# Routing in two phases: batches 0 to 3 inside attention's last groups, batches 4 to 7 behind it

## What is computed

```python
x = x + relu(xattn(layernorm(x), ctx, ctx) @ wo_w.T + wo_b)   # 16 heads of 16, 375 keys
xf = layernorm(x)                                             # 896 tokens x 256
scores = softmax(xf @ gw + gb)                                # 32 experts
group_scores = sum(top_k(scores.reshape(T, 8, 4), 2)[0])      # per group of 4 experts
keep = the 4 best groups
indices = top_k(where(keep, scores, -inf), 4)[1]              # 4 experts per token
weights = take_along_axis(scores, indices)
for e in range(32):
    h = silu(xf @ w1[e] + b1[e]) * (xf @ w3[e] + b3[e])
    y += cw[:, e] * (h @ w2[e] + b2[e])
z = silu(xf @ sw1 + sb1) * (xf @ sw3 + sb3) @ sw2 + sb2       # shared expert, 256 wide
return x + y + z
```

## Time and profile before

| | |
|---|---|
| time, median of 3 runs | 343.71 us (343.64 to 344.85) |
| the profiled execution: its run | 342.33 us |
| its span, first to last instruction | 340.6 us |
| PE busy | 300.8 us (88%) |
| DVE busy | 192.6 us (57%) |
| ACT busy | 158.0 us (46%) |
| POOL busy | 157.1 us (46%) |
| mean granted clock of PE | 0.94 |

### The profile page before, as it was taken

One profiled execution on the slowest core, in us unless ns is written; L12 is line 12 of the kernel. 1 busy time (PEld: TensorE's weight loads), 2 busy tenths in 40 slices (PEclk: granted clock), 3 DMA queues, 4 the chain that ended last, 5 costly groups with the idle time before them and its releaser, 6 DMA issues.

```text
span 340.6 us, 7222 instructions
## 1 busy us (share of the span) xinstructions
PE 300.8 (88%) x2311; PEld 209.3 (61%) x2311; DVE 192.6 (57%) x679; ACT 158.0 (46%) x426; POOL 157.1 (46%) x222
## 2 busy tenths in 40 slices
PE   7899999999999999899499646399999999999965
PEld 3566666666666677564445333267777777787543
DVE  2899766565656567178750301067876666666343
ACT  5566666666666656525011011045556665555101
POOL 7564444444444445001037777126555555555600
PEclk9999999999999999997679955599999999999999
DMA  7999596959786700008803333655544554553498
GB/s 193 214 155 307 164 315 191 297 146 318 228 250 195 244 2 2 0 2 243 253 28 100 110 113 111 107 110 181 156 149 150 162 157 154 162 158 107 129 295 210
DMA packets 56941, 55.92 MB, mean 164 GB/s; under 512 B 19165, under 2 KB 49386, under 8 KB 56394
## 3 DMA queue, kind: packets, MB, share of 16 engines
q1 hardware_dynamic: 52538, 43.94, 48.7%
q0 software_dynamic: 4368, 11.52, 10.3%
HBM read 35.03 MB, written 20.41 MB: 163 GB/s over the span
## 4 chain that ended last, share of the span: by engine, by line
PE 28%; POOL 9%; DVE 7%; DMA 5%; issue 4%; ACT 1%; DVEq 0%; SPq 0%; POOLq 0%
PE ps L961 13%; POOL expert_rows L879 9%; PE ps L976 6%; PE ps L953 3%; DMA b<-expert_out 2%; PE ps L970 2%; DMA expert_out<-hs,to 1%; PE ps L1016 1%; DMA expert_rows<-normed,slots 1%; DMA xg<-expert_rows 1%; POOL expert_out L884 1%; DVE hb L1234 1%; ACT sg L1050 1%; DVE hh L1240 1%; PE ps L924 1%
## 5 line engine op out<-in xcount | busy, mean ns | idle before, releaser
L607 DVE CUSTOM_DVE_ANT_0 z<-ps,mask_sb 112x375 f32<-112x375 f32 x128 | 62.5, 546 | 43.3 <-PE ps L390 43.2
L313 POOL TENSOR_SCALAR z<-z,zmax 112x375 f32<-112x375 f32 x96 | 55.7, 594 | 67.0 <-DVE zmax L607 67.0
L884 POOL DMA_INDIRECT expert_out<-hs,to x59 | 56.7, 961 | 51.2 <-DVE hs L1206 36.3
L513 ACT ACTIVATE pT<-ps 125x336 f32<-125x336 f32 x128 | 50.7, 448 | 38.5 <-PE ps L367 38.2
L961 PE MATMUL ps<-w,xgT 128*128 x236 | 65.6, 403 | 3.0 <-ACT xgT L1040 3.0
L367 PE MATMUL ps<-ident,z 112*125 112x112 f32 x384 | 56.6, 283 | 0.2 <-ACT pT L513 0.2
L367 PEld LDWEIGHTS ps<-ident,z 112*125 112x125 f32 x384 | 47.3, 188 | 14.9 <-ACT pT L513 7.3
L1234 DVE TENSOR_TENSOR hb<-ps,b 128x256 f32<-128x256 f32 x59 | 25.1, 425 | 52.0 <-PE ps L961 48.8
L961 PEld LDWEIGHTS ps<-w,xgT 128*128 128x128 f32 x236 | 43.9, 198 | 14.7 <-issue 6.7
L879 POOL DMA_INDIRECT expert_rows<-normed,slots x32 | 30.3, 947 | 29.4 <-DVE normed L1183 20.0
L1056 ACT COPY hs<-ps 128x128 f32<-128x128 f32 x59 | 15.6, 265 | 47.4 <-PE ps L970 47.4
(11 more groups left out here) (181 smaller groups left out, 346.0 us busy)
## 6 DMA issues: line engine op xcount, KB each, us to landing
xg<-expert_rows SPq DMA_DIRECT2D x59, 128.0 KB, 2.3
expert_rows<-zero SPq DMA_DIRECT2D x14, 512.0 KB, 10.1
w2s<-in_L_ffn_w SPq DMA_DIRECT2D x2, 2048.0 KB, 9.2
b<-in_L_ffn_b SPq DMA_DIRECT2D x2, 2048.0 KB, 13.2
ctx_sb<-in_ctx SPq DMA_DIRECT2D x8, 336.0 KB
b<-expert_out SPq DMA_DIRECT2D x6, 448.0 KB, 6.4
mask_sb<-in_mask_Bx1xSxS_ff SPq DMA_DIRECT2D x8, 164.1 KB, 2.3
expert_out<-hs,to POOLq DMA_INDIRECT x59, 2.8
```

The costliest lines, as they stand in the source:

```text
L313: pool.tensor_scalar(z[:, n % RING, :], z[:, n % RING, :], -1.0, zmax[:, n % RING:n % RING + 1], ALU.mult, ALU.add).then_inc(by_pool, 1)
L513: nc.scalar.activation(pT[:, n % RING, :], ps[0:KP, T_BANK + at % 2, 0:KT * S], ACT.Exp).then_inc(ring_read, 1)
L607: nc.vector.tensor_tensor_reduce(out=z[:, n % RING, :], in0=ps[0:S, S_BANK + j, 0:SK], in1=mask_sb[:, b % 2, :], scale=-1.0, scalar=BIG, o ...
L884: pool.indirect_dma_start(ys, bass.IndirectOffsetOnAxis(ap=to[:, j:j + 1], axis=0), y_sb[:, j % 4, :], None).then_inc(y_sent[j % 4], 16)
```

## The change

Routing is split into phase 0 (batches 0 to 3) and phase 1 (batches 4 to 7), with tiles of half the width.

- Phase 0 runs in attention. DVE takes mean and variance with the Newton steps in group 20 and normalises four batches in group 21; PE turns them as two ring units at the end of group 22 (`xT0`, `xT1`) and makes the logits as a third in 23; DVE's routing steps are dealt over groups 24 to 31, with ACT's exp in group 25; ranks and counts are a fourth unit at the end of group 31. Behind group 32's residual DVE makes blocks, keys and slots of phase 0.
- POOL issues 8 of the 16 scatters of phase 0 ahead of the barrier, 8 behind it. Its constants are made in group 5, DVE's tables in group 7.
- Phase 1 runs in `experts`. Its rows first fill what is free in an expert's last block of phase 0 (`room`) and then go to further blocks (`more_blocks`, `more_keys`). The number of blocks in the loop, 59, stays. A block's owner is the sum of two parts, one for each phase.
- `x_sb` is now the same tile as `x2`, and `wo_raw`, `b1r`, `b3r` lie in `xf`.

```diff
+    PHASES = ((0, B // 2), (B // 2, B))
+    PB = B // 2
+    ROUTED_AT = (("xT0", 22), ("xT1", 22), ("logit", 23), ("rank", 31))
+    EXP_AT = 25
+    FIRST_ROWS = 8
...
     def closing(p):
         b, r = p // QPB, p % QPB
+        units = []
         if p < NQ and r < 3 and b + 1 < B:
-            return [(("k0", "k1", "q")[r], b + 1)]
+            units.append((("k0", "k1", "q")[r], b + 1))
         if p < NQ and r == 3 and b:
-            return [("ctxT", b - 1)]
-        return []
+            units.append(("ctxT", b - 1))
+        return units + [(kind, 0) for kind, at in ROUTED_AT if at == p]
...
+        def more_blocks(chained, counts):
+
+            chained(nc.vector.scalar_tensor_tensor(base1[:], held[:], -1.0, counts, ALU.add, ALU.add))
+            chained(TT(over[:], base1[:].unsqueeze(2).to_broadcast([P, E, LIM]),
+                       full[:].unsqueeze(1).to_broadcast([P, E, LIM]), ALU.is_gt))
+            chained(nc.vector.tensor_reduce(blocks[:], over[:], AX.X, ALU.add))
+            chained(TT(shift[:], blocks[:], had[:], ALU.subtract))
+            chained(nc.vector.tensor_tensor_scan(ends[:], ones_e[:], shift[:], 0.0, ALU.mult, ALU.add))
+            chained(nc.vector.tensor_scalar(free[:, 1:2], ends[:, E - 1:E], -1.0, free[:, 0:1], ALU.mult, ALU.add))
+            chained(nc.vector.tensor_scalar(ends[:], ends[:], free[:, 1:2], None, ALU.add))
+            chained(TT(shift[:], ends[:], blocks[:], ALU.subtract))
+            nc.vector.scalar_tensor_tensor(base1[:], shift[:], float(PART), held[:], ALU.mult, ALU.add)
+            chained(nc.vector.scalar_tensor_tensor(tail1[:], shift[:], -float(PART), tail1[:], ALU.mult, ALU.add))
+
+        def more_keys(chained, ranks):
+            lo, hi = PHASES[1]
+            chained(TT(msc[:], ranks, every(room[:]), ALU.is_lt))
+            TT(msc[:], msc[:], every(tail1[:]), ALU.mult)
+            chained(TT(key[:, lo:hi, :], ranks, every(base1[:]), ALU.add))
+            chained(TT(key[:, lo:hi, :], key[:, lo:hi, :], msc[:], ALU.add))
+            chained(TT(key[:, lo:hi, :], key[:, lo:hi, :], sel[:, lo:hi, :].bitcast(F32), ALU.mult))
...
+        def place(chained, f):
+            lo, hi = PHASES[f]
+            sort_best(chained, f, key[:, lo:hi, :])
+            nc.vector.tensor_scalar(slots[:, lo:hi, :], best[:, lo:hi, 0:TOPK], -1.0, None, ALU.add).then_inc(slots_ok, 1)
+            nc.vector.tensor_scalar(normed[:, lo:hi, D:D + TOPK], best[:, lo:hi, 0:TOPK], -1.0, None, ALU.add).then_inc(slots_ok, 1)
...
+        def rank_and_count(f, ranks, counts):
+
+            lo, hi = PHASES[f]
+            nc.tensor.matmul(ranks, earlier[:, 0:ranks.shape[0]], sel[:, lo:hi, :].rearrange("s b e -> s (b e)"), start=True, stop=True)
+            for b in range(PB - 1):
+                ins = nc.tensor.matmul(ranks[:, (b + 1) * E:PB * E].rearrange("s (b e) -> s b e", e=E), ones[:, 0:ranks.shape[0]],
+                                       sel[:, lo + b:lo + b + 1, :].to_broadcast([S, PB - 1 - b, E]), start=False,
+                                       stop=True, skip_group_check=True)
+            ins.then_inc(ranked, 1)
+            for b in range(lo, hi):
+                ins = nc.tensor.matmul(counts, ones[:], sel[:, b, :], start=(b == lo), stop=(b == hi - 1))
+            return ins
...
+        EARLY_ROWS = [(r, b) for r in reversed(range(TOPK)) for b in range(*PHASES[0])]
...
+                    elif p == QPB + 1:
+                        routing_constants()
+                pool.wait_ge(slots_ok, 2)
+                pool.wait_ge(xs_zero, 16 * (N_ZERO + 1))
+                for r, b in EARLY_ROWS[:FIRST_ROWS]:
+                    scatter_rows(pool, r, b)
 
...
+                def turn_normed(k):
+                    bank = bank_of((f"xT{k}", 0))
+                    pe.wait_ge(xn_ok, PB)
+                    for b in range(PB):
+                        ins = nc.tensor.transpose(bank[:, b * S:(b + 1) * S], normed[:, b, k * P:(k + 1) * P], ident[0:S, 0:S])
+                    ins.then_inc(ring_full, 1)
+
+                def first_logits():
+                    unit = ("logit", 0)
+                    bank_of(unit)
+                    pe.wait_ge(ring_read, UNIT["xT1", 0] + 1)
+                    for b in range(PB):
+                        ins = route(pe, b, T_BANK + UNIT[unit] % 2)
+                    ins.then_inc(ring_full, 1)
+
+                def first_ranks():
+                    bank = bank_of(("rank", 0))
+                    pe.wait_ge(ones_ok2, 4)
+                    pe.wait_ge(sel_ok, 1)
+                    rank_and_count(0, bank[:, 0:PB * E], bank[:, PB * E:(PB + 1) * E]).then_inc(ring_full, 1)
...
-                for c, own_batches in ((0, range(0, B // 2)), (1, range(B // 2, B - 1))):
-                    pe.wait_ge(xn_ok, own_batches.stop)
-                    for k in range(DK):
-                        for b in own_batches:
-                            at = (b - own_batches.start) * S
-                            ins = nc.tensor.transpose(ps[:, 2 * c + k, at:at + S], normed[:, b, k * P:(k + 1) * P], ident[0:S, 0:S])
-                        ins.then_inc(xT_full, 1)
+                pe.wait_ge(xn_ok, B - 1)
+                for k in range(DK):
+                    for b in range(PB, B - 1):
+                        ins = nc.tensor.transpose(ps[:, k, (b - PB) * S:(b - PB + 1) * S], normed[:, b, k * P:(k + 1) * P], ident[0:S, 0:S])
+                    ins.then_inc(xT_full, 1)
 
                 pe.wait_ge(sums_ok, B)
-                for b in range(B - 1):
-                    if b in (0, B // 2):
-                        pe.wait_ge(xf_by_act, 2 if b == 0 else 4)
+                pe.wait_ge(xf_by_act, 2)
+                for b in range(PB, B - 1):
                     route(pe, b)
...
+                        if j == 2 and p == EXP_AT:
+                            act.wait_ge(lmax_ok, 1)
+                            nc.scalar.activation(ex[:], lg[:], ACT.Exp).then_inc(probs_ok, 1)
...
+                    if p == 7:
+                        tables(then_wait)
+                    if p == 20:
+                        aggregate(0, PB)
+                        newton(0, PB)
+                    if p == 21:
+                        for b in range(PB):
+                            normalise(b, x2, xn_ok)
+                    if p == 24:
+                        dve.wait_ge(ring_read, UNIT["logit", 0] + 1)
+                        lower_logits(then_wait, lg[:])
+                    if p == EXP_AT:
+                        dve.wait_ge(probs_ok, 1)
+                        softmax(then_wait)
+                        pairs_of_groups(then_wait)
+                    if p == 26:
+                        group_scores(then_wait)
+                    if p == 27:
+                        dve.wait_ge(const_ok, 5)
+                        dve.wait_ge(ones_ok2, 4)
+                        sort_best(then_wait, 0, gs[:])
+                        against_limit(then_wait, 0, gs[:], GROUPS, KEEP_GROUPS)
+                        count_equals(then_wait, GROUPS, restart_g)
+                        then_wait(take(then_wait, keep[:], GROUPS, KEEP_GROUPS))
+                    if p == 28:
+                        kept_scores(then_wait)
+                    if p == 29:
+                        sort_best(then_wait, 0, msc[:])
+                        against_limit(then_wait, 0, msc[:], E, TOPK)
+                    if p == 30:
+                        count_equals(then_wait, E, restart)
+                    if p == 31:
+                        take(then_wait, sel[:, 0:PB, :], E, TOPK).then_inc(sel_ok, 1)
+                        dve.wait_ge(sel_ok, 1)
+                        chosen_weights(0)
+                dve.wait_ge(ring_read, UNIT["rank", 0] + 1)
+                first_blocks(then_wait, ranks1[:, PB * E:(PB + 1) * E])
+                first_keys(then_wait, ranks1[0:S, 0:PB * E].rearrange("s (b e) -> s b e", e=E))
+                place(then_wait, 0)
+                variances(PB, B - 1)
+                first_state(then_wait, ranks1[:, PB * E:(PB + 1) * E])
                 divide(B - 1)
-                variances(0, B - 1)
-                inverses(0, B - 1, 2)
-                for b in range(B - 1):
+                inverses(PB, B - 1, 2)
+                for b in range(PB, B - 1):
                     normalise(b, x2, xn_ok)
+                owners(then_wait, 0)
...
+                for r, b in EARLY_ROWS[FIRST_ROWS:]:
+                    scatter_rows(pool, r, b)
+                pool.wait_ge(slots_ok, 4)
                 for r in reversed(range(TOPK)):
-                    for b in range(B):
-                        pool.indirect_dma_start(xs, bass.IndirectOffsetOnAxis(ap=slots[:, b, r:r + 1], axis=0),
-                                                normed[:, b, :], None).then_inc(scattered[r], 16)
+                    for b in range(*PHASES[1]):
+                        scatter_rows(pool, r, b)
...
-                pe.wait_ge(sel_ok, 1)
```

(16 more changed lines are left out.)

387 lines of the change are left out of this document (225 added, 162 removed).

## The result

The changed kernel takes **332.80 us** (median of 4 runs, 332.15 to 333.38) against 344.14 us for the kernel before on the same chip (343.64 to 344.85): a ratio of 0.9665, 95% interval 0.9637 to 0.9692. Of the twelfth experiment's four runs one was 1.6% above the fastest, a slower state that executions of any kernel can fall into, and it is left out of that experiment's time. The profiled execution of after has a span of 331.6 us in a run of 333.38; before it was 340.6 us in 342.33. The spans differ by 9.0 us. The forecast change was -9.7 us: the spans moved by 0.7 us less than that, the medians by 1.6 us more.

A forecast was written before the change was run, and what follows sets the result against it. It took POOL's 32 scatters to bound the stretch up to block 3, PE the rest. Barrier +5.8, down products -7.8 and row waits -7.7 gave -9.7 us: median 334.0 us, range 329.5 to 339.6.

The forecast's parts named there:

- Bounds: POOL's 32 indirect scatters bound the stretch from 174.65 us to block 3's turn; PE bounds the 122.4 us behind it.
- Part 1: Attention's last groups on PE get longer by 4.9 us (3.5 to 8) through four new ring units and DVE's steps.
- DVE's share: Groups 20 and 21: DVE's overrun delays masks and costs attention 0.45 us, with 0 and 3 as ends.
- The four normalisations: Group 21: by the port rule alone, beside POOL, they cost DVE 4 x 1.0 us, inside attention's upper end of 8.
- Part 2: The barrier waits for POOL's eight early scatters: release at 158.65 instead of 152.84, +5.8 us (+4 to +9).
- Part 3: Second routing behind the barrier, at half width, is shorter: sel at +10.05 us from release instead of +13.8.
- Down products: PE starts them at +18.7 us behind the release instead of +26.5, full clock kept: -7.8 us.
- the rival of half clock: PE stays at half clock through the second shared units: -5.4 in place of -7.8, 336.4 us; chance 0.22.
- Late first phase: DVE makes phase 0's slots 3 to 5 us later and POOL holds the barrier: 337 to 339 us; chance 0.13.
- Scatters held up by DVE: All eight scatters ahead of the barrier take 1.16 us instead of 0.94: +1.6, 335.6 us; chance 0.05.
- More gain: Blocks 0 to 2 follow without pause and the clock rises before block 3, up to 4 us: 330 us; chance 0.09.
- Slower: Groups 20 to 31: all 13.2 us of added DVE steps reach PE through late masks: 346.8 us; chance 0.07.

The follow-up runs named there:

- twelfth experiment: Changed kernel plus five unread 512-column products at the end of PE's attention part: 331.71 us, ratio 0.9653.
- fourth experiment: Changed kernel with phase 0 still routed early, but all 32 scatters issued behind the slots of phase 1: 340.7 us, ratio 0.9895.
- fifth experiment: Changed kernel with DVE's routing steps of groups 26, 28, 29 and 30 bunched into group 27: 339.31 us, one run.
- seven: Changed kernel with four scatters ahead of the barrier and PE's 15 register loads dealt out among the down products: 324.32 us, ratio 0.9444.
- eight: Four scatters ahead, PE's loads dealt out, and DVE's additions placed behind nine of its 15 register loads: 325.59 us, ratio 0.9450.
- eleven: Changed kernel plus eight unread 512-column products at the end of PE's attention part: 336.66 us, ratio 0.9794.
- experiments one: Changed kernel with no scatter ahead of the barrier instead of eight: 327.83 us, ratio 0.9503.
- two: Changed kernel with four scatters ahead of the barrier instead of eight: 329.27 us, ratio 0.9570.
- nine: Four scatters ahead, PE's loads dealt out, plus seven unread fill products behind the down products and ahead of blocks 0 to 3: 321.45 us, ratio 0.9321.
- ten: Changed kernel with no scatter ahead of the barrier and PE's register loads among the down products: 325.01 us, ratio 0.9441.
- six: Changed kernel with POOL explicitly waiting, ahead of the barrier, until its eight scatters have landed: 333.72 us, one run.

## Why the prediction was right, point by point

- **Bounds.** Right. With the 16 scatters of phase 0 moved, the waits for rows are gone; with them moved back (the fourth experiment) 12.9 us return.
- **The number.** The terms miss by up to 1.2 us each, and the sum by 0.7 us (-9.0 for -9.7), because they miss both ways: attention and its slots came early, the lag of the barrier, `sel` and the down products late. That much is luck. The path is as predicted, with three steps wrong in it, named below: the release, the slack of the masks, and PE's clock for batch 7.
- **Part 1, attention: +4.9, measured +3.7** (3.19 at group 31's scores and 3.73 at the first turn behind it). xT 1.47 for 1.8: ACT's copy of the queries held up xT1 by 0.34 us, but nothing queued behind the copies. Logits 1.69 for 1.7. Ranks 0.54 for 0.7. Exp 0 for 0.2. DVE's share 0.19 for 0.45: the masks of group 21 come 1.02 us late for some 1.3, and PE absorbs most of it. But "nearly a group of slack", the reason given for 0.45, is wrong: the slack is 0.8 us there and 1.0 in the fifth experiment, in a group of some 4. The terms for PE's own work were right.
- **The four normalisations** took 1.62 us together, not 1.42 each as the one in the earlier trace rows. POOL's lowerings of that group ended at 97.54, and only the first of the four, from 97.04, overlapped them: it took 0.65 us and ended 0.15 us behind POOL, and the three others took 0.40 each. The one of the earlier trace rows ended 0.15 us behind a copy of POOL's in the same way (33.89 and 33.74). The rule on shared ports (Trainium skill, SBUF — State Buffer, "Who interferes with whom") has whoever comes second wait for the whole instruction of the other. The trace agrees, and it costs 0.25 us here and not the 4 x 1.0 of the upper end, since POOL had no more work.
- **Part 2, the barrier: +5.8, measured +6.8.** Slots came at about 147.1 instead of 148.2, and eight scatters took 9.9 us as computed (147.40 to 157.33). The step that failed is the last one, "release at 158.65": I gave 0.25 us between POOL's end and the release, and it is 2.33. The early slots (1.1 us) take back about half of the lag (2.1).
- **Part 3, the second routing: `sel` at +10.05, measured +10.9.** Missing was that PE is at half clock for batch 7 behind the barrier, which I had considered only for later places. The price is 0.55 us by the twelfth experiment, and all kernels bear it out: where these logits took 0.95 us `sel` came at +10.66 to +10.91, where they took 0.58 (experiments four, seven, eight, eleven and twelve) at +10.27 to +10.38. The 5.3 us of idling are not needed for it: in experiments one, two, nine and ten PE idled 0.48 us at the barrier, and the logits took 0.95 as well. The remaining 0.3 us was not traced.
- **Down products at +18.7, measured +19.15; -7.8, measured -7.35.** In the profiled execution PE kept full clock over its 1.04 us of idling, as predicted, and the rival of half clock (336.4) did not come. But the reason that I gave, "under 1 us idle", isn't a safe one: with waits of 1.08, 1.17 and 1.58 us full clock was kept (experiments four, seven and ten), with 1.19 and 1.24 (eight and six) it fell, and the down products then start up to 1.4 us later. The rival deserved its 0.22.
- **Block 0 at +37.9, measured +38.05. Block 3 at +49.9, measured +49.83.** No wait for rows; -7.7, measured -7.9. Behind it 122.1 us for 122.4.
- **The rivals.** *Late first phase*: no, the slots were early. *Scatters held up by DVE*: the first took 1.16 us again, as in every kernel wherever it stands, the fifteen others of phase 0, which ran beside DVE's steps, 0.94 to 0.98 (single ones up to 1.06 in experiments two and nine); it fell. *More gain*: the clock of blocks 0 to 2 stayed at half, so not in this kernel; that the mechanism is worth about 3 us between blocks 0 and 3 was shown by the fill (11.07 to 8.16 us). *Slower*: it didn't come, but the bunched steps show its mechanism. Its price of one for one holds beyond DVE's idle time in the group and about 1 us of slack, and a fall of PE's clock can come on top. The reason that I gave against it, DVE's idle time per group, is the right measure.
- **Not seen ahead**: the eight scatters in front of the barrier are a loss. My own sum had it (+5.8 for the barrier, and 8 us of the scatters' gain lying idle), but I asked only what the change does and not which part of it pays. With 0 or 4 instead of 8 the time is 3.5 to 5 us lower.

## What to carry to other kernels

Before work is moved ahead of a barrier, ask whether its engine will then be the last to arrive, and whether anyone behind wants the result that early: here about 1.25 us for each scatter that outlasted DVE, and the 2.3 us lag behind the last, were paid at the barrier, and none of it came back. Steps put into an in-order queue that feeds the bottleneck are free up to the queue's idle time in each round and a little slack (here 0.8 to 1.0 us) and cost one for one beyond it, so deal them out by rounds and read the idle time round by round, not as a sum. When an engine's pause is "issue", look for instructions without busy time, and put them between queued work.

## What the runs showed of the hardware that I had not expected

- Behind the last of 8 or 16 indirect scatters POOL let a barrier go only 2.3 to 2.65 us after its record ended (2.33, 2.32 and 2.31 us with 8, 2.65 with 16); with four, whose last ended 2.2 us before DVE's last work did, none of it was seen. Waiting explicitly for the landing made it 2.93.
- Fifteen register loads cost PE 5.45 us in one piece; dealt out among matmuls they gave 3.6 of these back. DVE's fifteen filled the 10.28 us of idling ahead of its additions; with nine of them ahead it was 6.46 us.
- PE's clock in the products behind the ranks: 1.00 where PE had idled 0.98, 1.04, 1.08, 1.17 and 1.58 us for `sel`, a fall to 0.50 within some two microseconds where it had idled 1.19 and 1.24, and 2.87 twice, with the same products after it. A pause of about a microsecond can go either way, also between executions of the same code. Pauses of 0.66 to 1.26 us ahead of the first blocks' products went with 0.50, and the same stretch with fill in it and pauses of 0.49 and 0.61 left kept 1.00.
